# A four-stage network on one core: a new timetable for the selective scan, a reciprocal root on ScalarE in the router, and sums by rows in the combine stage

## The reference

```python
xz = x @ W_in.T                          # Mamba: 512 channels, 16 states
xc, z = jnp.split(xz, 2, axis=-1)
xc = silu(conv4(xc))                     # causal, 4 taps
dbc = xc @ W_xproj.T                     # dlt (16), B (16), C (16)
delta = softplus(dlt @ W_dt.T + b_dt)
h = exp(delta * A) * h + delta * B * xc  # over the 2048 positions, per channel and state
y = sum over states(h * C) + xc * D
out = (y * silu(z)) @ W_out.T
...
scores = softmax(x @ gate_w.T)           # experts: the router
topk_w, topk_ids = top_k(scores, 8)
y = (rows of the 8 experts * topk_w).sum(axis=1)
x = layernorm(x + y)                     # (r - mean) / sqrt(var + eps)
```

## Time and profile before

| | us |
|---|---|
| median of three runs | 5063.2 (5061.3 to 5067.9) |
| the profiled execution | 5056.7, its span 5054.9 |
| scan stage, DVE's first scan to its last product | 61 to 1062 |
| tree layer, projections and attention | 1062 to 3725 |
| router | 3725 to 4110 |
| experts | 4110 to 4890 |
| combine | 4892 to 5053 |

### The profile page before, as it was taken

One profiled execution on the slowest core, in us unless ns is written; L12 is line 12 of the kernel. 1 busy time (PEld: TensorE's weight loads), 2 busy tenths in 40 slices (PEclk: granted clock), 3 DMA queues, 4 the chain that ended last, 5 costly groups with the idle time before them and its releaser, 6 DMA issues. The chain is left out here.

```text
span 5054.9 us, 84397 instructions
## 1 busy us (share of the span) xinstructions
PE 4342.6 (86%) x20410; PEld 3064.2 (61%) x20411; DVE 3700.1 (73%) x7521; ACT 2830.2 (56%) x6544; POOL 1747.8 (35%) x1517
## 2 busy tenths in 40 slices
PE   6887787769999879999999999999976649999960
PEld 2333333336666447888888888888865637777740
DVE  6999999966666678888888888888854433333349
ACT  6777777522222118888888888888843314444420
POOL 5777777620000011122121212122137743333321
PEclk8999999999999989999999999999987869999985
DMA  1000000021111461211121112212135445555558
GB/s 42 13 13 13 13 13 9 9 69 36 36 36 35 151 188 26 52 31 49 27 58 26 50 26 59 51 26 51 34 116 169 164 127 157 156 150 155 156 174 276
DMA packets 329081, 384.68 MB, mean 76 GB/s; under 512 B 124209, under 2 KB 263337, under 8 KB 323003
## 3 DMA queue, kind: packets, MB, share of 16 engines
q1 hardware_dynamic: 255931, 265.05, 17.8%
q0 software_dynamic: 26112, 73.44, 4.1%
q10 hardware_dynamic: 46944, 45.16, 3.3%
HBM read 230.26 MB, written 153.24 MB: 76 GB/s over the span
## 5 line engine op out<-in xcount | busy, mean ns | idle before, releaser
L1539 DVE TENSOR_TENSOR probsT<-ps_t,probsT 128x512 fp32r<-128x512 f32 (+3 forms) x1280 | 779.6, 609 | 137.8 <-ACT probsT L1479 116.2
L1479 ACT ACTIVATE probsT<-ps_t 128x512 fp32r<-128x512 f32 (+3 forms) x1280 | 686.6, 536 | 255.8 <-PE ps_t L1327 231.2
L1471 ACT ACTIVATE probs<-ps_s,negm 128x512 f32<-128x512 f32 (+3 forms) x1297 | 812.4, 627 | 28.1 <-DVE negm L1532 27.1
L1339 PE MATMUL ps_o<-probsT,vbuf 128*128 128x512 f32 (+3 forms) x2560 | 815.8, 402 | 6.8 <-ACT folding L1485 6.2
L1314 PE MATMUL ps_s<-kbuf,qbuf 128*128 (+1 forms) x2602 | 768.7, 380 | 59.2 <-ACT probs L1471 31.5
L1519 DVE TENSOR_REDUCE pmax<-ps_s 128x1 f32<-128x512 f32 (+3 forms) x1301 | 777.6, 600 | 48.6 <-PE ps_s L1314 24.3
L1327 PE MATMUL ps_t<-idn,probs 128*128 128x128 f32 x4352 | 694.8, 275 | 13.8 <-DVE probsT L1539 13.8
L445 POOL TENSOR_TENSOR dBx<-u,b_all 128x1024 f32<-128x1024 f32 x256 | 616.2, 2409 | 237.0 <-DVE h L531 226.3
L1327 PEld LDWEIGHTS ps_t<-idn,probs 128*128 128x128 f32 x4352 | 517.4, 142 | 135.2 <-DVE probsT L1539 41.0
L1314 PEld LDWEIGHTS ps_s<-kbuf,qbuf 128*128 128x128 f32 x2602 | 445.5, 189 | 179.0 <-issue 65.4
L1422 POOL CAST qbuf<-qstage 128x512 fp32r<-128x512 f32 x132 | 81.4, 616 | 1272.1 <-DMA qstage<-q_scr 748.1
(11 more groups left out here) (249 smaller groups left out, 7243.5 us busy)
## 6 DMA issues: line engine op xcount, KB each, us to landing
xr<-xs ACTq DMA_DIRECT2D x294, 136.0 KB
parts<-y SPq DMA_DIRECT2D x36, 1024.0 KB, 5.2
qstage<-q_scr SPq DMA_DIRECT2D x528, 64.0 KB
w_gu<-W_guT SPq DMA_DIRECT2D x64, 384.0 KB, 3.5
q_scr<-rot SPq DMA_DIRECT2D x64, 256.0 KB, 2.9
attn<-ostage SPq DMA_DIRECT2D x128, 128.0 KB, 2.0
at<-attn SPq DMA_DIRECT2D x32, 512.0 KB, 4.1
w_d<-W_downT SPq DMA_DIRECT2D x64, 192.0 KB, 3.7
```

Of the source, the lines that this page charges most:

```text
L1339: last = nc.tensor.matmul(ps_o[:, lo:], vbuf[:, kb, :, :], probsT[:, g % SLOTS, part, lo:], start=kb == 0 and part == 0, stop=kb == BAND * ...
L1471: nc.scalar.activation(probs[:, k, at:at + n, :], ps_s[:, u % RING, 0:n * P], ACT.Exp, bias=negm[:, tile, :], accum_out=sums[:, s, j, c:c ...
L1479: nc.scalar.activation(probsT[:, g % SLOTS, 0, lo:], ps_t[:, t % 2, lo:], ACT.Copy).then_inc(high_t.sem, 1)
L1539: nc.vector.tensor_tensor(probsT[:, g % SLOTS, 1, lo:], ps_t[:, t % 2, lo:], probsT[:, g % SLOTS, 0, lo:].bitcast(F32), ALU.subtract).then ...
```

## The change

In the scan stage:

- In four units of each chunk (v = 18, 20, 25, 27, `SHARED_AT`) the product hc = h x C is no longer DVE's but POOL's. POOL can't read PSUM, so ACT first copies `ps_c` to the new SBUF tile `c_sb` (`take_c`, behind the unit's first `decay`). POOL's product stands before `drive` of the loop's next step. PE's next `spread_c` waits for ACT's copy, its `sum_states` for POOL's product, and DVE's scan of unit q + 2 for POOL's product of unit q (it reuses `h`).
- The skip products move from state 1 of each half to v = 13 and 24 (`SKIP_AT`).
- SiLU of z's first half moves from v = 2 to v = 1.
- The x projection is split: two of its four matmuls at v = 16, two at v = 18.
- Before the loop: `first_taps` goes block by block instead of tap by tap, ACT's first SiLU waits for the first two blocks only, the x projection is split likewise, and delta of the second half is made after the first scan.

In the router 1/sqrt leaves POOL: ACT makes exp(-0.5 x ln(var + eps)) in two instructions, behind `take_attn`, and DVE refines it by a Newton step in three, in front of its `norm`.

In the combine stage the nine rows are added by rows: DVE rows 0 to 3 (`add_low`, 128x512), POOL rows 4 to 8 (`add_high`, 128x512 and 128x256), DVE both results (`add_quarters`, 128x512, and `add_last`, 128x256). POOL's part of tile t + 2 stands behind its 1/sqrt of tile t.

```diff
+    SHARED_AT = (18, 20, 25, 27)
+    SKIP_AT = (13, 24)
...
-                pe.wait_ge(hc_done.sem, hc_done.at(q))
+                if shared(q):
+                    pe.wait_ge(c_taken.sem, shared_no[q])
+                else:
+                    pe.wait_ge(hc_done.sem, q + 1 - shared_no[q])
                 if q + 1 < UNITS:
                     spread_c(q + 1)
+                if shared(q):
+                    pe.wait_ge(hc_shared.sem, shared_no[q])
                 sum_states(q)
...
+            def take_c(q):
+                act.wait_ge(c_ready.sem, c_ready.at(q))
+                if shared_no[q] > 1:
+                    act.wait_ge(hc_shared.sem, shared_no[q] - 1)
+                nc.scalar.activation(c_sb[:, 0, :], ps_c[:, 0, :], ACT.Copy).then_inc(c_taken.sem, 1)
...
+            def weigh(q):
+                pool.wait_ge(c_taken.sem, shared_no[q])
+                pool.wait_ge(scan_done.sem, scan_done.at(q))
+                pool.wait_ge(reduce_done.sem, reduce_done.at(q - 2))
+                nc.gpsimd.tensor_tensor(hc[:, q % 2, :, :], h[:, q % 2, :, :], c_sb[:, :, :].to_broadcast((P, DH, TC)),
+                                        ALU.mult).then_inc(hc_shared.sem, 1)
...
+                if q and shared(q - 1):
+                    weigh(q - 1)
                 if q + 2 < UNITS:
                     drive(q + 2)
...
+                if q >= 2 and shared(q - 2):
+                    dve.wait_ge(hc_shared.sem, shared_no[q - 2])
...
             low_parts(0)
-            for hv in range(HALVES):
-                make_delta(0, hv)
+            make_delta(0, 0)
             for q in range(UNITS):
...
                 scan(q)
+                if q == 0:
+                    make_delta(0, 1)
...
-                weigh(q)
+                if not shared(q):
+                    weigh(q)
...
+            def inv_std(t):
+                h = t % 2
+                act.wait_ge(aggr.sem, aggr.at(t))
+                nc.scalar.activation(log[:, h, :], mv[:, h, 1:2], ACT.Ln, bias=eps_sb[:, :]).then_inc(log_done.sem, 1)
...
+                nc.scalar.activation(guess[:, h, :], log[:, h, :], ACT.Exp, scale=-0.5).then_inc(guessed.sem, 1)
...
             for t in range(NT):
-                if t + 3 < NT:
-                    inv_std(t + 3)
                 pool.wait_ge(copied.sem, copied.at(t))
...
+            def add_high(t, s, loads):
...
+                nc.gpsimd.tensor_tensor(high[:, h, :, :], parts[:, s, HALF:HALF + 2, :], parts[:, s, HALF + 2:TOPK, :], ALU.add
+                                        ).then_inc(half_done.sem, 1)
+                pool.wait_ge(half_done.sem, half_done.at(t))
+                nc.gpsimd.tensor_tensor(high[:, h, 0, :], high[:, h, 0, :], parts[:, s, TOPK, :], ALU.add).then_inc(high_done.sem, 1)
...
+                nc.vector.tensor_tensor(low[:, s % 2, :, :], parts[:, s, 0:2, :], parts[:, s, 2:HALF, :], ALU.add
+                                        ).then_inc(low_done.sem, 1)
...
+                nc.vector.tensor_tensor(low[:, s % 2, :, :], low[:, s % 2, :, :], high[:, s % 2, :, :], ALU.add
+                                        ).then_inc(quarter.sem, 1)
```

More of the change, by code:

```diff
@@ L153, in carries, with shared @@
             return q // STEPS % PER_SEQ < PER_SEQ - 1
+        def shared(q):
+            return q % STEPS in SHARED_AT
+        shared_no = list(itertools.accumulate([int(shared(q)) for q in range(UNITS)]))
         carry_no = list(itertools.accumulate([int(carries(q)) for q in range(UNITS)]))
@@ L247, in _ @@
             pe.wait_ge(consts.sem, 16 * CONSTS)
-            x_proj(0)
+            for hv in range(HALVES):
+                x_proj(0, hv)
             for d in range(DB):
@@ L397, in _ @@
                 decay(DH * q + RING)
+                if shared(q):
+                    take_c(q)
                 if v == 0:
@@ L497, in first_taps @@
             def first_taps():
-                for t in range(TAPS):
-                    for j in range(DB):
+                for j in range(DB):
+                    for t in range(TAPS):
                         if t == 0:
@@ L526, in scan @@
                     dve.wait_ge(carry_done.sem, carry_no[q - 2])
+                if q >= 2 and shared(q - 2):
+                    dve.wait_ge(hc_shared.sem, shared_no[q - 2])
+                elif q >= 2 and shared(q - 1):
+                    dve.wait_ge(hc_done.sem, q - 1 - shared_no[q - 2])
                 dve.wait_ge(dbx_done.sem, dbx_done.at(q))
@@ L1648, in route @@
         rstd = sb("rstd4", [P, 2, 1])
-        nhalf = sb("nhalf4", [P, 1])
+        log = sb("log4", [P, 2, 1])
+        guess = sb("guess4", [P, 2, 1])
+        square = sb("square4", [P, 2, 1])
+        part = sb("part4", [P, 2, 1])
         eps_sb = sb("eps4", [P, 1])
@@ L1716, in route @@
         aggr = tally("aggr4")
-        add = tally("add4")
-        pw = tally("pow4")
+        log_done = tally("log4_done")
+        guessed = tally("guessed4")
+        newton = tally("newton4", 3)
         x3_ready = tally("x3_ready")
@@ L1935, in _ @@
             nc.gpsimd.memset(xe[:, :, :, DM + 2:ROW], 0.0).then_inc(pad_set.sem, 1)
-            pool.wait_ge(nh_set.sem, 3)
-            for t in range(3):
-                inv_std(t)
             pool.wait_ge(pad_set.sem, 1)
@@ L2411, in combine @@
         parts = sb("parts", [P, SLOTS, TOPK + 1, DM])
+        low = sb("low6", [P, 2, 2, DM])
+        high = sb("high6", [P, 2, 2, DM])
         r4 = sb("r4", [P, 2, DM])
@@ L2478, in total, with add_last @@
+            def add_last(t, s):
+                dve.wait_ge(quarter.sem, quarter.at(t))
                 dve.wait_ge(o_ready.sem, o_ready.at(t - 2))
-                cols = slice(half * DM // 2, (half + 1) * DM // 2)
-                nc.vector.reduce_sum(r4[:, s % 2, cols], parts[:, s, :, cols].rearrange("p k d -> p d k"),
-                                     axis=mybir.AxisListType.X).then_inc(summed.sem, 1)
+                nc.vector.tensor_tensor(r4[:, s % 2, :], low[:, s % 2, 0, :], low[:, s % 2, 1, :], ALU.add).then_inc(summed.sem, 1)
@@ L2483, in _ @@
             o_ready.credit(dve)
-            for half in range(2):
-                total(0, 0, 1, half)
+            quarter.credit(dve)
+            add_low(0, 0, 1)
+            add_quarters(0, 0)
+            add_last(0, 0)
             with dve.Fori(0, NT // SLOTS) as i:
                 for s in range(SLOTS):
-                    t, h = SLOTS * i + s, s % 2
-                    following = (t + 1, (s + 1) % SLOTS, i + 1 + (s + 1) // SLOTS)
+                    t, h, nxt = SLOTS * i + s, s % 2, (s + 1) % SLOTS
```

98 lines of the change are left out of this document (65 added, 33 removed).

## The result

The changed kernel takes 4973.6 us (median of four runs, 4967.8 to 4979.9) against 5062.2 us (median of four runs of the kernel before, 5056.1 to 5067.9): ratio 0.9825, 95% interval 0.9808 to 0.9842. It is 1.75% faster. The forecast was 4958; the time lies in the range of 4924 to 4997. The profiled execution took 4979.9 us (span 4977.7), 77 us less than the profiled one before, where the steps had given 104. It is the slowest of its four; by the medians the gain is 89 us.

A forecast was written before the change was run, and what follows sets the result against it. DVE bounds the scan and combine stages, POOL the router; gains of 55.5 (scan), 25 (router) and 23.5 (combine) sum to 104 us, giving 4953 profiled, 4959 as median; forecast 4958, 8-in-10 range 4924 to 4997.

The forecast's parts named there:

- The three bounds: The scan stage is bound by DVE, the router by POOL (11.09 us a tile), the combine stage by DVE (4.70 us a tile).
- v = 4: Scan stage: DVE's wait there for ACT's exp, 15.5 us in all, goes; 14 us saved (bounds 8 and 15.5).
- v = 19: Scan stage: DVE's wait for the spread C behind the x projection goes; all 13.5 us saved, including small waits at v = 3.
- Before the loop: Ahead of the scan loop: shorter wait for taps (about 7 us) and an earlier first scan (2.4); 9.5 us saved.
- Delta: Scan stage: DVE's delta at v = 27 meets POOL's half-done drive, about 1 us in seven chunks; 7 us lost.
- - 11 (slow PE clock at hand-over): Scan stage: at slow PE clock DVE waits about 2.5 us in a little over half the chunks; 11 us lost.
- The step of v = 20: Scan stage: after POOL's product, PE's sum, dt_proj and C are ready at 15.4, needed at 15.5; slow, about 2.5 us wait.
- the moved products: Scan stage: four of 32 products leave DVE, 32 x 1.14 = 36.5 us saved if nothing new is waited for.
- The rival in which the hand-overs eat the moved products: Scan stage: POOL a drive late, DVE waits about 1.2 us per product, 36.5 us gone; total 4995 us, chance 0.2.
- Router: Router: POOL saves 0.91 us for each of 28 tiles, first tiles lose 1 us; 25 us saved (bounds 15 and 26).
- Combine: Combine stage: 4.0 us a tile as DVE and POOL take turns; 23.5 us saved (bounds 6 and 46).
- normalising at 1.45 to 1.85: Combine stage: DVE normalises in 0.4 us while POOL's 128x512 sum runs from 1.45 to 2.7; statistics follow to 2.2.

## Why the prediction was right, and where it was off

**What held.** The three bounds, the sign, the range, and the order of the stages. v = 4: 14.1 us, forecast 14. v = 19: gone, 13.5 with the small waits at v = 3. Before the loop: the first product starts 9.2 us sooner, forecast 9.5; DVE then waits 0.57, 0.86 and 0.69 us for C and an exp that used to be ready, so that its fourth product is 7.2 us ahead. The first scan itself starts at 48.8, sooner than the forecast 51 to 54; DVE then stands 1.9 us until it can make the second delta, in front of the first product. The products of 18 and 20 by POOL were in time, and DVE never waited for `h`. Delta was longer: 4.1 us for the forecast 7, of which 2.6 at v = 27 and 1.5 at v = 31.

**The term that failed in the scan stage** is "- 11 (slow PE clock at hand-over)". Measured: 29.9, of which 15.3 at v = 22 to 24 (the step itself, mis-sized: 2.9 us each instead of 2.5, in five chunks), 6.1 at v = 26, 6.6 at v = 29 and 30, and the rest at v = 1 and 2. The step of v = 20 has a slip of its own: it counts the sum of unit 20 as 1.3 us, and 12.1 + 1.3 + 1.1 + 0.5 is 15.0, not the 15.4 that it gives. The sum takes 1.9 us at full clock (377.69 to 379.60) and 3.7 at half (131.50 to 135.21), so 15.4 is right as a time and the "twice 2.9" is too little: 6.5 us were measured. The prediction had stepped through v = 18 to 22 and had stopped there; at 25 it named a thin cover for the rival only, and did not follow the skip products, which its own sum counts as gone from state 1, to where they arrived. Against it stands a term too small: the moved products gave 42 us, not 36.5. Together 42 + 14.1 + 13.5 + 9.2 - 29.9 - 4.1 = 44.8, and 44.7 was measured; that it closes this well is partly luck, since the same scan code varies by some 4 us. The rival in which the hand-overs eat the moved products was half right in its amount: of 42 us 11.3 were left, where it had none left and the forecast 18.5. Its mechanism was another: it had POOL a `drive` late, while DVE waited for PE's C.

**Router.** 29.5 us against 25, above the term and its upper bound of 26, for two small reasons: a tile takes 10.12 us and not 10.18, where it took 11.10 before (0.98 x 28 = 27.4), and two tiles that took 12.48 us each before have no counterpart now (2.8). The first tiles cost 1.0 us, as forecast. DVE's Newton step and ACT's pair stayed hidden.

**Combine.** 12.6 us against 23.5. The step that failed is "normalising at 1.45 to 1.85": it was counted as an instruction that POOL's sum doesn't touch. POOL's 128x512 sum had been made to hold DVE's low sum ("to 3.3"); it held the instruction in front of it, and the 0.4 us of statistics, which were to run beside it, came behind it as well (4888.66). Only the smaller sum, 0.73 us, was left to hold the low one. With 4.26 us a tile instead of 4.0 the tiles gave 13.8 us; the first normalisation came 0.7 us sooner after the first load, and the end of the stage, from the last normalisation on, took 5.16 us where it took 3.28: 12.6.

**The other stages** lost 9.6 us in the profiled run without a changed instruction; the forecast had put them at nothing. Some 4 us of it is at the start of the tree layer, where the clock comes back later after PE's idle stretch: the first two blocks of L783 take 9.39 and 8.80 us, in the kernel before 7.08 and 7.11, with a granted clock of 0.72 and 0.83 in the windows of 10 us where it was 0.96 and 1.00.

```profile
1040.89 9.39 PE L783 MATMUL ps_l<-f_in,x1T 128*128 128x510 f32 x16 [0.52 <-issue]
...
1054.98 8.80 PE L783 MATMUL ps_l<-f_in,x1T 128*128 128x510 f32 x16 [2.74 <-ACT x1T L837]
```

The rest was not located. From the last gate to the router's first transfer the changed kernel took 2699.8 us, its twelve variants 2692 to 2701, the kernel before 2689.2 in its one profile. That it varies is shown; why, and whether the kernel before is always shorter there, is not. Nor is it shown what makes the 89 us of the medians out of the 77 of the profiles.

**The total.** The forecast of 104 us of gain was 15 too high by the medians and 27 by the profiles. The errors are -10.8 (scan), -9.6 (other stages), +4.5 (router) and -10.9 (combine): only the router's made up for another. The median lies in the range, and in the narrower one of the forecast's own case (4940 to 4980), because these were wide enough for the misses, not because each stage was hit; that the medians differ by 12 us more than the profiles helped.

## What to carry to other kernels

When work moves from the bounding engine to an idle one, step through the hand-over for every place where it happens, and follow what is queued on the third engine behind it; here a product placed where a fill kept TensorE busy was worth its full 1.3 us, and one placed where GpSimd was behind with its work 0.3. Where GpSimd works out of SBUF beside VectorE instructions with two SBUF tensors, or a float32 `tensor_scalar` of one, look for them waiting for each other, and count their lengths as one queue where they do. The operand of a small VectorE instruction that starts beside a long one of GpSimd may be better off in PSUM: one line shortened the combine stage by 23 us, as long as the loads kept up.
